# Moving a chunk's outputs one step later on ScalarE, and the tail of a fused Mamba and feed-forward kernel into both arms of a branch

## The reference

```python
x = x + layernorm(attn(layernorm(x)))
x = x + layernorm(ffn(layernorm(x)))
```

```python
r = sigmoid(xr @ W_r.T); k = xk @ W_k.T
out = r * (square(relu(k)) @ W_v.T)
```

## Time and profile before

| | |
|---|---|
| median of three runs | 269.48 us (269.29 to 269.48) |
| the profiled execution, its own time | 269.2 us |
| its span, first to last instruction | 267.4 us |
| mean granted TensorE clock | 0.972 |
| busy: PE, DVE, ACT, POOL | 226.0, 209.4, 190.0, 156.0 us |

### The profile page before, as it was taken

One profiled execution on the slowest core, in us unless ns is written; L12 is line 12 of the kernel. 1 busy time (PEld: TensorE's weight loads), 2 busy tenths in 40 slices (PEclk: granted clock), 3 DMA queues, 4 the chain that ended last, 5 costly groups with the idle time before them and its releaser, 6 DMA issues.

```text
span 267.4 us, 6587 instructions
## 1 busy us (share of the span) xinstructions
PE 226.0 (85%) x1958; PEld 173.9 (65%) x1958; DVE 209.4 (78%) x637; ACT 190.0 (71%) x727; POOL 156.0 (58%) x267
## 2 busy tenths in 40 slices
PE   0995987799999989999999899899989997868560
PEld 0984434568787778788688668687868786455350
DVE  1799999977789979759989889898989876545531
ACT  2458657689876888778779877977798777663641
POOL 6423407587886986858686667576666844242101
PEclk9997999999999999999999999999999999997886
DMA  5960000000000000000000100010010001001103
GB/s 130 221 231 2 0 0 1 0 4 0 5 2 0 2 1 2 0 5 1 2 2 0 44 0 2 0 44 0 4 30 13 0 2 39 7 7 39 42 6 73
DMA packets 10169, 6.48 MB, mean 24 GB/s; under 512 B 832, under 2 KB 9824, under 8 KB 10128
## 3 DMA queue, kind: packets, MB, share of 16 engines
q1 hardware_dynamic: 9984, 5.77, 8.6%
q0 software_dynamic: 144, 0.21, 0.4%
HBM read 3.88 MB, written 2.10 MB: 22 GB/s over the span
## 4 chain that ended last, share of the span: by engine, by line
PE 47%; ACT 19%; issue 13%; DVE 11%; POOL 5%; DMA 2%; ACTq 1%; POOLq 1%; DVEq 0%
PE bank L862 10%; PE bank L943 5%; PE bank L764 5%; PE bank L856 5%; PE pair L850 4%; ACT xn L661 4%; ACT bt L601 3%; PE bank L731 3%; ACT bank L590 3%; PE bank L968 3%; PE bank L967 3%; PE bank L976 2%; PE bank L978 2%; ACT junk L579 2%; ACT o_all L692 2%
## 5 line engine op out<-in xcount | busy, mean ns | idle before, releaser
L590 ACT ACTIVATE bank<-bank,rsn 128x512 f32<-128x512 f32 x32 | 21.1, 658 | 22.8 <-PE bank L764 22.7
L1211 DVE TENSOR_TENSOR x<-bank,wx 128x512 f32<-128x512 f32 x32 | 22.0, 686 | 18.8 <-ACT bank L590 16.9
L862 PE MATMUL bank<-x,sg 64*64 64x256 f32 x256 | 34.6, 385 | 0.0
L862 PE MATMUL bank<-xg,sg 64*64 64x256 f32 x256 | 33.8, 376 | 0.0
L850 PE MATMUL pair<-x,turned_bc 64*64 64x256 f32 x224 | 29.6, 376 | 0.0
L459 POOL TENSOR_TENSOR y<-ysum,zs 128x256 f32<-128x256 f32 x32 | 23.4, 732 | 10.1 <-DVE ysum L1234 10.0
L856 PE MATMUL bank<-st,bt 64*64 64x256 f32 x128 | 20.8, 395 | 6.6 <-ACT bt L601 5.8
L432 POOL TENSOR_TENSOR frs<-fmo,halfn 128x8 f32<-128x8 f32 (+1 forms) x10 | 13.8, 1383 | 19.5 <-DVE fmo L1301 16.7
L392 POOL TENSOR_TENSOR rb<-mse,halfn 128x2 f32<-128x2 f32 x32 | 23.5, 734 | 2.5
L364 POOL TENSOR_TENSOR x_lo<-xnT_all,x_hi 128x128 fp32r<-128x128 f32 x32 | 14.7, 460 | 17.6 <-ACT x_hi L505 17.4
L862 PEld LDWEIGHTS bank<-xg,sg 64*64 64x64 f32 x256 | 21.4, 133 | 4.8
(11 more groups left out here) (185 smaller groups left out, 757.4 us busy)
## 6 DMA issues: line engine op xcount, KB each, us to landing
x_all<-x SPq DMA_DIRECT2D x16, 128.0 KB, 3.8
out<-o_all SPq DMA_DIRECT2D x16, 128.0 KB, 2.4
cm<-consts SPq DMA_DIRECT2D x1, 640.0 KB, 5.3
w_sb<-w_in SPq DMA_DIRECT2D x1, 480.0 KB, 4.2
cm<-consts POOLq DMA_DIRECT2D x1, 128.0 KB, 4.0
wo_sb<-w_out SPq DMA_DIRECT2D x1, 128.0 KB, 4.9
bcb_sb<-bc_bias SPq DMA_DIRECT2D x1, 96.0 KB, 3.4
wr_sb<-w_r SPq DMA_DIRECT2D x1, 64.0 KB, 4.6
```

The costliest lines, as they stand in the source:

```text
L590: nc.scalar.activation(x_ps[:], x_ps[:], ACT.Silu, scale=rsn[:, par:par + 1]).then_inc(S["x_silu"], 1)
L862: mm = nc.tensor.matmul(y_ps[half(h)], sg[half(h), a, r], rx(x, r)[half(h)], start=start, stop=stop)
L1211: vec.tensor_tensor((x1, xg)[a][:, par].rearrange("p (a e) -> p a e", e=P), x_ps[:].rearrange("p (a e) -> p a e", e=P), wx[:, par, a].unsq ...
```

## The change

Two edits. On ACT, outputs(c-4) moves from q = 1 to q = 2, and every engine's count of steps grows by one to reach it. On POOL, PE and DVE the loop over the remaining `ffn(n)` moves from behind the branch to the end of `tiles(general)`, so that it stands in both arms.

```diff
-FFN_STEPS = NT + 3 * NQ + 2
+FFN_STEPS = NT + 3 * NQ + 3
...
@@ gpsimd, at the end of tiles(general)
                     step(n, n % NQ, general)
+                for n in range(NT, FFN_STEPS):
+                    ffn(n)
...
             with pool.Else():
                 tiles(True)
-
-
-            for n in range(NT, FFN_STEPS):
-                ffn(n)
...
@@ scalar, ffn(n)
-                if q == 1 and valid(c - 4):
+                if q == 2 and valid(c - 4):
                     outputs(c - 4)
...
@@ tensor, at the end of tiles(general)
                     step(n, general)
+                for n in range(NT + 1, FFN_STEPS):
+                    ffn(n)
...
             with pe.Else():
                 tiles(True)
-            for n in range(NT + 1, FFN_STEPS):
-                ffn(n)
...
```

## The result

| | before | after |
|---|---|---|
| median of 4 runs, us | 269.38 (268.52 to 269.48) | 263.32 (260.90 to 265.87) |
| ratio, 95% interval | | 0.9707 [0.9643, 0.9771] |
| profiled execution, own time / span, us | 269.2 / 267.4 | 261.76 / 260.0 |
| mean granted TensorE clock of it | 0.972 | 0.982 |

The ratio compares undisturbed runs only and so leaves out the two longer executions of the changed kernel (264.89 and 265.87 us); the experiments show that their length is the kernel's own. By the ratio the change is worth 7.9 us, and by the two medians 6.1, against 4.9 forecast. A second measurement of the same kernel, six executions on another chip (E5), gave 0.9811 [0.9762, 0.9860], 5.1 us.

What follows compares the result with a forecast made beforehand. ACT was taken to set the pace in four q = 1 steps, and PE's jump to delay the tail. 4.32 - 0.1 + 0.58 = 4.8 us less gave a forecast of 264.5 us, range 262.7 to 266.3.

Steps and rivals of the forecast that it cites:

- ACT sets the pace in q = 1: Chunks 4 to 7, q = 1: without outputs PE sets the pace again, 27.24 to 22.92 us, gain 4.32 us.
- chunk 3's number: Length of chunk 3's q = 1 stretch, which has no outputs: 5.73 us, forecast for all four stretches.
- Outputs fit into q = 2: Chunks 4 to 6, q = 2: outputs fill ACT's wait and delay x_gate by 0 to 0.08 us each; 0.1 taken.
- The bound of 0.42 us: Possible loss if q = 3 stretches of chunks 4 to 6 took 6.69 us, not 6.55; kept for the range only.
- DVE covers the denser rhythm: DVE, busy 6.04 us in q = 1, can let work slip into q = 2 (4.33 of 5.26 busy): no cost.
- The jump: PE's 3.35 us jump no longer delays project_v(5): gain 0.58 us; POOL and DVE gain nothing; hidden at the end.
- the sum: Total gain of the forecast's terms: 4.32 - 0.1 + 0.58 = 4.8 us.
- The two rules on the branch: Taken branch out of the prefetched window stalls for a fetch; unconditional branch takes about 51 ns. The measured 3347 ns was used.
- The clock: PE's granted clock, low in parts of the tail: no term in the forecast, only rivals and the range.
- the rival on PE's clock in the tail: The shift spares one low-clock stretch (262.8 us) or adds one (266.0 us): chance 0.10, half each way.
- The price of a stretch: Cost of one low-clock stretch of PE in the tail: 43% of 3.74 us busy, 1.6 us.
- The prediction's last sign of being wrong: The forecast is wrong if granted clock below 1 covers more or less of the tail than before.

Runs made afterwards that it cites:

- E5: Changed kernel measured again, unaltered, on another chip: 264.45 us, ratio 0.9811 to the kernel before.
- E4: Kernel before, with 10 matmuls on constants in PE's tail gaps, too long for them: 268.50 us, ratio 0.9971.
- E7: Kernel before, with shorter matmuls on constants filling PE's gaps behind project_v and turn_normed in the tail: 266.38 us, ratio 0.9899.
- E9: Changed kernel with PE's tail gaps filled by short constant matmuls, and PE's tail alone put back behind the branch: 262.52 us, ratio 0.9757.
- E1: Kernel before with only outputs moved to q = 2 on ACT, tail still behind the branch: 263.38 us, ratio 0.9790.
- E2: Kernel before with only the tail moved into both arms on POOL, PE and DVE, outputs at q = 1: 267.81 us, ratio 0.9950.
- E6: Changed kernel, with short matmuls on constants filling PE's gaps behind project_v and turn_normed in the tail: 261.95 us, ratio 0.9727.
- E8: Kernel before with only outputs moved, plus short constant matmuls filling PE's tail gaps: 262.35 us, ratio 0.9738.
- E10: Kernel before with only the tail moved into the arms, plus short constant matmuls filling PE's tail gaps: 265.98 us, ratio 0.9876.
- E12: Changed kernel, with constant matmuls filling only PE's gaps ahead of project_k in the tail, those behind project_v left empty: 261.48 us, ratio 0.9713.

## Why the prediction was right or wrong

**ACT sets the pace in q = 1: right.** Expected 22.92 us for the four stretches; measured 3 x 5.73 + 5.88 = 23.07. The gain is 4.17 us where 4.32 was forecast. The 0.15 is chunk 7, whose x_gate again waited for PE (ACT is idle for 0.14 us before it). I had taken chunk 3's number for a stretch with other work in it. The prediction's reading that PE does the same 6.3 us of work in the long stretch was wrong: in the stretch without outputs PE is busy for 5.58 us, as in chunk 3, and only so can it last 5.73.

**Outputs fit into q = 2: right.** 0.01 us per chunk where I took 0.1 us for three. The q = 3 stretch stayed at 6.55 us; the 6.69 was a matter of single executions, since the kernel before shows 6.55 there in E4 and E7. The bound of 0.42 us wasn't needed.

**DVE covers the denser rhythm: right.** Its work slipped into the next stretch, as argued: 6.04 us became 5.07 in q = 1, and 4.33 became 5.18 of 5.27 us in q = 2, and nothing grew.

**The jump: mechanism right, size at its lower end, and not quite free at the end.** 0.58 us was the gap in the profiled execution; the runs show 0.58 to 1.25, since the jump takes 3.27 to 4.02 us. POOL's and DVE's share is nothing, as argued (E9). No engine's stall comes back at the end, but the last store gets up to 0.4 us longer there, 0.15 in the changed kernel; the sum had nothing for it.

**The two rules on the branch.** The rule of the Trainium skill's page "Runtime: NRT & Kernel Launch" (instruction fetch mechanics) on a taken branch out of the prefetched window agrees with every run: the jump's duration of over 3 us moved with it to 249.2 us, and one 16 KB packet of kind "instruction" lies in each jump. The 51 ns that the Trainium skill's page "Advanced Engine Details and Errata" (Control Flow Timing) gives is what DVE's branch row itself reads, at 231.50 in the kernel before, but DVE's next instruction starts only at 235.04. PE's jump rows read 3.27 us and more.

**The clock: wrong, and the step that failed.** The sum took the clock of the one profiled execution as a property of both kernels and so put its term at nothing, and the rival on PE's clock in the tail allowed for one low stretch more or less, at 0.05 each way. The price of a stretch was right (1.6 us forecast; (19.64 - 16.30) / 2 = 1.67 measured), its place a little off: 251.8 is where project_k(7) starts, and the clock falls at 252.58. But the low stretches in the tail differ from one execution to the next. The profiles of kernels without filling show three patterns: none (the changed kernel in the result), two of 3.4 us that cost 3.3 us together (the kernel before, and the changed kernel in E5), and one of 6.8 us that costs 2.6 (E1, E2). The result's ratio rests on two executions of the changed kernel at a granted clock of 0.982; the profiled one has no low stretch in the tail, and so 7.9 us show: 4.17 + 0.58 of the change and about 3.3 of clock. Without the clock the change is worth 4.43 us (E7 - E6), 0.4 less than the sum of 4.8. The medians of E5 and of the kernel before beside it differ by 5.1 us; that this is so near the forecast's 4.9 is in part luck, since some 0.7 us of it is the clock's. The trace of one execution couldn't tell the spread of the clock; three runs within 0.2 us made me take it for fixed. The prediction's last sign of being wrong, a low clock over more or less of the tail than before, is the one that came.

What stays open is what decides, in a given execution, whether the clock falls in the tail. E1 and E2 rule out the jump as the cause: with it and without it the clock stays up in some executions and falls in others. The record does say that the change makes a difference to the clock. Of the 46 executions of the kernel before whose granted clock is on record none reads over 0.978; of the 28 of the changed kernel, E1 and E2, six read 0.981 or 0.982. And without filling each part gains more than with it: 5.7 against 4.0 us for the outputs (E1; E7 - E8), 5.1 against 4.4 for both (E5; E7 - E6), 1.3 against 0.4 for the tail (E2; E7 - E10). The chips differ in the first and the last of these pairs, so the sizes are rough, and by what the parts spare the clock is not shown.

## What to carry to other kernels

Compare the same kind of step with and without the piece of work that moves; if the kernel already contains the step without it, its length is the forecast. Where PE has gaps ahead of work on the path (1.1 to 1.7 us here), read the granted clock of that stretch and count a fall of it as part of the spread, in both kernels. A few matmuls into an idle bank, shorter than the gap, made both kernels here faster and more even, but measure one of them first. The jump over an untaken arm took over 3 us on PE: let it stand behind the engine's last work, and compare the last store before and after.

## What was not expected of the hardware

Filling gaps of PE with useless matmuls took 3.2 us off the kernel before (269.57 to 266.38) and 2.5 us off the changed one (264.45 to 261.95). Filling the gap directly ahead of the costly matmuls was enough (E12). The same jump took between 3.27 and 4.02 us in fourteen profiles, and always ended 1.34 to 1.39 us after the one instruction packet of 16 KB that started in it. The last store took 2.40 us with no such packet beside it, and up to 2.78 with one or two of queue q14.
